# An attention layer with a feed-forward tail on one core: four heads at a time in the weighing, rounds of three score pairs and two units of fp32 work

## The reference

```python
h = layernorm(x) * (1 + ca) + sa
q = einsum('bnhd,hed->bnhe', h.reshape(B, N, 16, 16), Wq)
scores = einsum('bnhe,bmhe->bhnm', q, q) * 4      # / 16 ** -0.5
res = einsum('bhnm,bmhe->bnhe', softmax(scores), q)
x = x + ga * (res.reshape(B, N, 256) @ Wp.T + bp)
h = layernorm(x) * (1 + cb) + sb
# FFN: a second layernorm, w1 (256x1024, dequantised), silu, w2 (1024x256), residual
x = x + gb * (h + 0.5 * (silu((layernorm(h) * gamma + beta) @ w1 + b1) @ w2 + b2))
```

## Time and profile before

| | us |
|---|---|
| median of three runs | 2234.79 |
| profiled execution | 2229.72 |
| its span | 2227.4 |
| PE busy | 2010.8 (90%) |
| ACT busy | 1990.1 (89%) |
| DVE busy | 541.6 (24%) |
| mean granted clock of TensorE, share of full speed | 0.979 |

### The profile page before, as it was taken

The page is one execution under the profiler, slowest core; times in us unless marked ns, Lnnn a source line. Parts: engine busy times, 40 slices in busy tenths (PEclk is TensorE's granted clock), DMA queues, the critical chain, the costliest instruction groups (busy, mean ns, idle before and its releaser), DMA issues.

```text
span 2227.4 us, 34350 instructions
## 1 busy us (share of the span) xinstructions
PE 2010.8 (90%) x14087; PEld 598.4 (27%) x14087; DVE 541.6 (24%) x1289; ACT 1990.1 (89%) x2161; POOL 91.6 (4%) x42
## 2 busy tenths in 40 slices
PE   5578889899999999899998999999998999989995
PEld 3312222222322223222322223222332223222233
DVE  7513101421124211421014211322014211232113
ACT  2489999999998999999998999989998999989980
POOL 2000000100001000100001000000001000010001
PEclk9889999999999999999999999999999999999997
DMA  3251111111111111112111111111111111111000
GB/s 124 80 169 47 47 44 41 45 40 43 46 50 40 47 47 45 49 28 56 43 52 38 45 50 39 46 40 54 39 55 38 40 44 51 44 33 42 28 10 10
DMA packets 66572, 107.45 MB, mean 48 GB/s; under 512 B 15344, under 2 KB 49776, under 8 KB 66160
## 3 DMA queue, kind: packets, MB, share of 16 engines
q1 hardware_dynamic: 66416, 105.26, 16.2%
HBM read 96.56 MB, written 8.65 MB: 47 GB/s over the span
## 4 chain that ended last, share of the span: by engine, by line
PE 66%; ACT 15%; DVE 8%; issue 5%; DMA 0%; ACTq 0%; SPq 0%; DVEq 0%
PE attend_sums L700 34%; PE attend_scores L688 16%; ACT attend_probs L664 14%; PE attend_out L733 5%; PE attend_out L728 5%; DVE attend_sums_sb L818 3%; PE attend_sums L709 3%; PE attend_out L719 1%; ACT attend_half_tanh L653 1%; DVE attend_rsqrt_work L73 1%; DVE attend_rs L68 1%; PE attend_scores L728 1%; PE attend_scores L733 1%; DVE attend_st L847 1%; DVE z L873 0%
## 5 line engine op out<-in xcount | busy, mean ns | idle before, releaser
L664 ACT ACTIVATE attend_probs<-attend_scores 128x1024 f32<-128x1024 f32 x2048 | 1918.6, 1033 | 101.5 <-PE attend_scores L688 90.5
L700 PE MATMUL attend_sums<-attend_probs,values 128*17 128x512 f32 x8192 | 988.3, 600 | 0.2 <-ACT attend_probs L664 0.2
L688 PE MATMUL attend_scores<-asks,keys 64*128 64x512 f16 x4096 | 648.8, 384 | 85.3 <-ACT attend_probs L664 71.0
L688 PEld LDWEIGHTS attend_scores<-asks,keys 64*128 64x128 f16 x4096 | 151.6, 93 | 838.0 <-ACT attend_probs L664 681.8
L700 PEld LDWEIGHTS attend_sums<-attend_probs,values 128*17 128x17 f32 x8192 | 189.5, 97 | 467.2 <-issue 413.5
L818 DVE COPY attend_sums_sb<-attend_sums 128x512 f32<-128x512 f32 x128 | 88.5, 691 | 869.1 <-PE attend_sums L700 869.1
L733 PE MATMUL attend_out<-w,hidden 128*128 128x256 f32 x448 | 126.6, 405 | 0.0
L728 PE MATMUL attend_out<-attend_ffn_in,w 128*128 128x512 f32 x224 | 126.0, 645 | 0.0
L883 DVE TENSOR_SCALAR attend_half_in<-attend_out,b_col 128x512 f32<-128x512 f32 x56 | 42.0, 751 | 336.5 <-PE attend_out L728 336.5
L709 PE MATMUL attend_sums<-ident,attend_sums_sb 128*128 128x128 f32 x512 | 83.9, 286 | 35.3 <-DVE attend_sums_sb L818 35.3
L733 PEld LDWEIGHTS attend_out<-w,hidden 128*128 128x128 f32 x448 | 75.9, 189 | 45.1 <-issue 39.3
(11 more groups left out here) (130 smaller groups left out, 604.2 us busy)
## 6 DMA issues: line engine op xcount, KB each, us to landing
keys<-parts_dram SPq DMA_DIRECT2D x256, 128.0 KB
keys<-parts_dram SPq DMA_DIRECT2D x256, 64.0 KB
keys<-parts_dram SPq DMA_DIRECT2D x256, 56.0 KB
asks<-parts_dram SPq DMA_DIRECT2D x192, 64.0 KB
start_x_in<-L_attn_x SPq DMA_DIRECT2D x8, 512.0 KB, 6.3
parts_dram<-start_q_parts SPq DMA_DIRECT2D x16, 256.0 KB, 2.5
attend_x_now<-L_attn_x SPq DMA_DIRECT2D x8, 512.0 KB, 7.5
out<-attend_base SPq DMA_DIRECT2D x16, 256.0 KB, 5.8
```

Of the source, the lines that this page charges most:

```text
L664: act.activation(probs[n % P_RING], ps_scores[:, 2 * slot:2 * slot + 2, :], ACT.Exp, scale=scale)\
L688: last = pe.matmul(ps_scores[:, 2 * (n % S_RING) + b, :], keys[rows, hh % K_RING, j * P:(j + 1) * P], asks[rows, h, :], start=True, stop=True)
L700: last = pe.matmul(ps_sums[32 * q:32 * q + E1, :], values[:, tile, hh % H, :], probs[(4 * m + i) % P_RING][:, b, :], start=(d == 0 and i < ...
```

## The change

A *group* is now four heads, and the loop goes over 32 groups of 16 steps. A step is four pairs, one of each head, for the same two key tiles. The four column tiles of the weighing belong to the four heads. A *unit* is four matmuls, one for each head; two units make a step. Each tile then holds the complete sum of its head, so the addition of four quarters (L823) goes, and copy, transposes and division come once per group instead of once per head, with four heads in one division.

Keys come in parts: a part is a quarter of the keys of the four heads, and it takes eight DMAs where a head took six. `probs` has 12 slots.

TensorE's order is in rounds. A group of 64 pairs has 22 rounds, 20 of three pairs and two of two. Behind the pairs of a round stand two units of fp32 work: two units of the weighing in the even rounds, one unit and then one piece in the odd ones. Round 0 does the last two units of the group before, and round 1 has `turn_sums` and a piece. The pieces have 44 places per chunk instead of 48. Both norms are computed on VectorE directly after the last projection piece.

Below, `SIZES` are the pairs of each round, `UNITS` its units, `WEIGHED` their running sum.

```diff
+Q_HEADS = 4
+GROUPS = G * Q_GROUPS
+STEPS = TILES // 2
+PAIRS = STEPS * Q_HEADS
+S_RING, P_RING, K_RING = 3, 12, 4
+SIZES = [3] * 20 + [2] * 2
+UNITS = [0, 0] + [2 - r % 2 for r in range(2, len(SIZES))]
+PLACE_ROUND = range(1, len(SIZES), 2)
+TURN_ATT, PROJECT, TURN_Z2, UP, DOWN = 0, 2, 9, 11, 28
...
-                def weigh(m):
-                    hh, d = divmod(m, 4)
-                    if d == 0:
-                        pe.wait_ge(sums_cleared, 1) if hh == 0 else pe.wait_ge(quarters_added, hh)
-                    pe.wait_ge(exps_done, 4 * m + 4)
-                    for i in range(4):
-                        for b in range(2):
-                            q, tile = (2 * i + b) % 4, 4 * d + i + PAIRS * b
...
+                def weigh(gg, unit):
+                    j, b = divmod(unit, 2)
+                    if unit == 0:
+                        pe.wait_ge(sums_cleared, 1) if gg == 0 else pe.wait_ge(group_done, gg)
+                    if b == 0:
+                        pe.wait_ge(exps_done, gg * PAIRS + Q_HEADS * (j + 1))
+                    for hq in range(Q_HEADS):
+                        n = gg * PAIRS + Q_HEADS * j + hq
+                        last = pe.matmul(ps_sums[32 * hq:32 * hq + E1, :], values[:, j + STEPS * b, (gg % Q_GROUPS) * Q_HEADS + hq, :],
+                                         probs[n % P_RING][:, b, :], start=(unit == 0), stop=(unit == 2 * STEPS - 1))
+                    if b == 1:
+                        last.then_inc(steps_done, 1)
...
-                        if n % 2 == 0 and n >= P_RING:
-                            act.wait_ge(units_done, (n - P_RING) // 2 + 1)
+                        if n % Q_HEADS == 0 and n >= P_RING:
+                            act.wait_ge(steps_done, (n - P_RING) // Q_HEADS + 1)
...
-                for hh in range(HEADS):
-                    c, h = divmod(hh, H)
-                    for d in range(4):
-                        scores(hh, 4 * d)
-                        scores(hh, 4 * d + 1)
-                        if d == 1 and hh > 0:
-                            turn_sums(hh - 1)
-                        scores(hh, 4 * d + 2)
-                        if c > 0 and d != 1:
-                            out_piece(c - 1, slot_of(h, d))
-                        scores(hh, 4 * d + 3)
-                        if hh > 0 or d > 0:
-                            weigh(4 * hh + d - 1)
...
+                for gg in range(GROUPS):
+                    c, group = divmod(gg, Q_GROUPS)
+                    for r in range(len(SIZES)):
+                        for p in range(STARTS[r], ENDS[r]):
+                            scores(gg, p)
+                        if r == 0 and gg > 0:
+                            for unit in range(WEIGHED[-1], 2 * STEPS):
+                                weigh(gg - 1, unit)
+                        if r == 1 and gg > 0:
+                            turn_sums(gg - 1)
+                        for unit in range(WEIGHED[r] - UNITS[r], WEIGHED[r]):
+                            weigh(gg, unit)
+                        if r in PLACE_ROUND and c > 0:
+                            out_piece(c - 1, group * SLOTS + r // 2)
...
-                    dve.tensor_reduce(whole, ps_sums.rearrange("p (t q e) -> p t e q", t=GT, q=4)[:, :, 0:E1, :],
-                                      AX.X, ALU.add).then_inc(quarters_added, 1)
-                    dve.wait_ge(quarters_added, hh + 1)
-                    dve.reciprocal(inverse, whole[:, :, E]).then_inc(inverse_ready, 1)
...
+                    dve.reciprocal(inverse, turned[:, :, :, E]).then_inc(inverse_ready, 1)
```

More of the change, by code:

```diff
@@ L27 @@
 REACH = 120.0
[L29 to L33, removed]
-RSQRT_STEPS = 12
+Q_HEADS = 4
+Q_GROUPS = H // Q_HEADS
+GROUPS = G * Q_GROUPS
+STEPS = TILES // 2
+PAIRS = STEPS * Q_HEADS
+S_RING, P_RING, K_RING = 3, 12, 4
+K_STEPS = STEPS // 4
+K_PAIRS = K_STEPS * Q_HEADS
+FILL_K, FILL_Q = 16 * 8, 16 * 10
+RSQRT_STEPS = 12
+SIZES = [3] * 20 + [2] * 2
+ENDS = [sum(SIZES[:r + 1]) for r in range(len(SIZES))]
+STARTS = [0] + ENDS[:-1]
+UNITS = [0, 0] + [2 - r % 2 for r in range(2, len(SIZES))]
+WEIGHED = [sum(UNITS[:r + 1]) for r in range(len(SIZES))]
+PLACE_ROUND = range(1, len(SIZES), 2)
+SLOTS = len(PLACE_ROUND)
+TURN_ATT, PROJECT, TURN_Z2, UP, DOWN = 0, 2, 9, 11, 28
 class Scope:
@@ L385, in adaln_layer, with load_keys @@
             "shift_set", "shift_turned", "split_step", "shift_stored"))
-        def load_keys(eng, hh):
-            h, slot = hh % H, hh % K_RING
+        def load_keys(eng, part):
+            group, quarter = divmod(part, 4)
+            head, slot = (group % Q_GROUPS) * Q_HEADS, part % K_RING
             for b in range(2):
[L391 to L395, removed]
+                first = b * HALF + quarter * K_STEPS * P
+                by_head = parts_dram[:, head * E:(head + Q_HEADS) * E, first:first + K_STEPS * P].rearrange("s (h e) n -> s e h n", e=E)
+                rows = keys[64 * b:64 * b + 64, slot, :, :]
+                eng.dma_start(rows[0:E], by_head[0]).then_inc(k_in[slot], 16)
+                eng.dma_start(rows[E:2 * E], by_head[0]).then_inc(k_in[slot], 16)
+                eng.dma_start(rows[2 * E:3 * E], by_head[1]).then_inc(k_in[slot], 16)
+                eng.dma_start(rows[3 * E:3 * E + KEEP], by_head[1, 0:KEEP]).then_inc(k_in[slot], 16)
         def load_asks(eng, c, group):
@@ L550, in adaln_layer @@
         sums_sb = a.take("sums_sb", BANK)
-        inverse = a.take("inverse", GT)
-        whole = a.take("whole", GT * E1).rearrange("p (t e) -> p t e", t=GT)
+        inverse = a.take("inverse", GT * Q_HEADS).rearrange("p (t h) -> p t h", t=GT)
         st2 = a.take("st2", GT * 6).rearrange("p (t s) -> p t s", t=GT)
@@ L591, in _ @@
                 load_shifts(sp, 0, 0)
+                load_keys(sp, 2)
+                load_keys(sp, 3)
                 for group in range(1, Q_GROUPS):
-                    load_keys(sp, group + 1) if group + 1 < K_RING else None
                     load_asks(sp, 0, group)
@@ L606, in _ @@
                 load_x(sp, 0)
-                for hh in range(HEADS):
-                    c, h = divmod(hh, H)
[L609 to L615, removed]
+                for part in range(4 * GROUPS):
+                    sp.wait_ge(scores_ready, K_PAIRS * (part + 1))
+                    if part + K_RING < 4 * GROUPS:
+                        load_keys(sp, part + K_RING)
+                    c, within = divmod(part, 4 * Q_GROUPS)
+                    if within % 4 == 3 and c + 1 < G:
+                        load_asks(sp, c + 1, within // 4)
+                        load_shifts(sp, c + 1, within // 4)
+                    if within == 0 and c > 1:
                         sp.wait_ge(y_ready, 2 * (c - 2) + 2)
                         store_y(sp, c - 2, 1)
-                    if h == 8 and c > 0:
+                    if within == 8 and c > 0:
                         sp.wait_ge(x1_ready, 2 * c)
                         load_x(sp, c)
-                    if h == 13 and c > 0:
+                    if within == 14 and c > 0:
                         sp.wait_ge(y_ready, 2 * (c - 1) + 1)
@@ L665, in _ @@
                            .then_inc(exps_done, 1)
-                        if c > 0 and (h, j) in tanh_after:
-                            tanh(c - 1, tanh_after[h, j])
+                        if c > 0 and (group, p) in tanh_after:
+                            tanh(c - 1, tanh_after[group, p])
                 o = G - 1
@@ L676, in _, with scores @@
                 pe.wait_ge(kappa_set, 2)
[L678 to L684, removed]
+                def scores(gg, p):
+                    n = gg * PAIRS + p
+                    c, group = divmod(gg, Q_GROUPS)
+                    j, hq = divmod(p, Q_HEADS)
+                    part = n // K_PAIRS
+                    if n % K_PAIRS == 0:
+                        pe.wait_ge(k_in[part % K_RING], FILL_K * (part // K_RING + 1))
+                    if p == 0:
+                        pe.wait_ge(q_in[group], FILL_Q * (c + 1))
@@ L685, in scores @@
                     wait(pe, exps_done, n - S_RING + 1)
                     for b in range(2):
-                        rows = slice(64 * b, 64 * b + 64)
-                        last = pe.matmul(ps_scores[:, 2 * (n % S_RING) + b, :], keys[rows, hh % K_RING, j * P:(j + 1) * P],
-                                         asks[rows, h, :], start=True, stop=True)
+                        rows, col = slice(64 * b, 64 * b + 64), (j % K_STEPS) * P
+                        last = pe.matmul(ps_scores[:, 2 * (n % S_RING) + b, :], keys[rows, part % K_RING, hq, col:col + P],
+                                         asks[rows, group * Q_HEADS + hq, :], start=True, stop=True)
@@ L708, in turn_sums @@
+                def turn_sums(gg):
+                    pe.wait_ge(sums_copied, gg + 1)
                     for t in range(GT):
@@ L944, in _, with after_tanh @@
+                def after_tanh(o, s):
```

(2 more changed lines are left out.)

183 lines of the change are left out of this document (75 added, 108 removed).

## The result

| | before | after |
|---|---|---|
| median (4 runs each), us | 2233.44 | 2153.99 |
| range, us | 2229.79 to 2237.96 | 2153.62 to 2154.42 |
| span of the profiled execution, us | 2227.4 | 2151.0 |

The ratio is 0.9644, with a 95% interval of 0.9628 to 0.966: 79 us less, 3.6% faster. The forecast was 2140 (2105 to 2175).

The account below looks back on a forecast made before the run. By stage, PE bounded the chunks with pieces, an ACT-PE loop chunk 0. Seven chunks at 244.7 us plus 236.2 make 1949.1 against 2040.85, 91.7 less; 2229.7 - 91.7 = 2138, given as 2140, range 2105 to 2175.

Parts of the forecast that it names:

- Middle of a group: Double rounds of three pairs each, six exps: 5.70 us with a piece, 5.50 without; ACT idle about 0.2 us.
- step s: TensorE's step between unit and piece, shown by no row of before: taken as 0.11 us, between 0 and 0.30.
- free step: Step s at 0, its lower end; the sum would be some 18 us lower.
- dear one: Rival: step s at 0.30 us at some 31 places per chunk, 34 us more, 2174; chance 0.11.
- The seam: Rounds 20 and 21, two pairs each but full blocks: 4.25 us for the last four exps; 3.9 in a chunk's first group.
- From exp 58: Chain reckoned at the seam from this exp: 6.25 us for six exps, two (2.0) already counted, so 4.25 for four.
- The norm's wait: Once per chunk, the wait for the second norm (z2) and the low clock behind it, 4.8 us, would go.
- cover: From last projection piece to z2's first: 20.9 us, VectorE needing 19.1, so the norm is in time by 1.8 us.
- At nothing: DVE's copies, additions and divisions, 12 slots of `probs`, and two more DMAs per part were put at no cost.

Follow-up runs that it names:

- first experiment: Kernel before, with POOL's three additions for `base` started after the second norm instead of beside it: 2196.0 against 2232.9 us, ratio 0.9844.
- second against first: Second: kernel before, with copy, transposes and division of the sums only at every fourth head, 2191.5 us, ratio 0.9817; set against the first experiment.

## Why the prediction was right, and where it was off

The direction, the mechanism and the range were right; the gain was 79 us where 94 was forecast.

*Middle of a group: right.* 5.70 forecast and 5.71 measured with a piece, 5.50 and 5.51 without. The step s = 0.11 was measured as 0.11, so neither the free step nor the dear one came true. ACT's idle time in these double rounds is 0.10 us, at the first exp of a round, where about 0.2 was expected.

*The seam: the term that was mis-sized.* The prediction counted "From exp 58", that is, it let the second pair of round 20 wait for exp 58, as third pairs do. But a round of two pairs comes to this wait when exp 58 is over: in the group shown exp 58 ends at 594.70, the first pair starts at 595.29 and the second at 595.52. PE arrives late and not ACT. The right sum is PE's work alone, from figures that the prediction had: 0.54 + 1.84 + 0.54 + 2.04 = 4.96 for four exps instead of 4.25. The 0.71 in three groups and 0.34 in the first (4.24 for 3.9) make 2.5 of the 2.95 us by which a chunk missed, some 17 us in all. The rest is spread over the double rounds, such as the 5.77 behind each seam and, in the third group, rounds with a tanh. That PE has no pause in the timeline, and that one unit less takes its whole 0.86 from the seam, shows that this work is what counts there.

*The norm's wait: right*, in cause and nearly in size (4.5 for 4.8 per chunk). The cover of 2.0 us held. The weighing behind the wait is 1.76 times as long as usual (3.36 against 1.91), not quite doubled; the granted clock over it is 0.55 on average, so nearly all of it ran at the lower level.

*At nothing: right for what was said, but one thing was missed.* PE never waits for keys in the chunks; that the form of the old DMAs held up the store of the bounds, and that 3.5 us would be won before the first exp, I had not seen. By luck it made up for a part of the seam.

Taken apart by the runs, the 76.4 us of the two spans are: 31.5 for the norm's wait (first experiment), 9 for the turns (second against first: 6.4 and 2.6), 31 for rounds in threes in place of blocks of four (1761.9 to 1731.9 in chunks 1 to 7, 238.1 to 236.8 in chunk 0), 4 before the first exp, and under 1 in the tail. The order of the first two parts matters: rarer turns alone take away the norm's wait too, 41 us together, so in the changed kernel that wait may be gone by the grouping, by the moved norms, or by either. The third part is a difference of two kernels and holds the four-head order too; an order of rounds without the grouping was not tried. What the grouping brings by itself is therefore not shown.

Still open is why the changed kernel ran at 2154.0 in one set of runs and at 2158.0 in another, while the profiled executions of both (2153.6 and 2154.7) are nearly alike. In the second set two of the five are at 2154.6 and 2154.7 and three at 2158 to 2160.

## What to carry to other kernels

Where two engines feed each other through a short ring, write down the loop from a release over the block behind it to the next supply, and beside it the plain sum of the work; the larger one counted here at both places, and in the short rounds it changed from the loop (5.70 against a sum of 5.40) to the sum (4.96 against a loop of 4.25). A cost in a chain can be hidden by its neighbour's catching up, so take it out alone before crediting it. And look for the one wait with a low clock behind it first: here one moved semaphore in the kernel before brought 37 us, where the whole change brought 79.

## What the hardware showed that I had not expected

- Some small instructions on VectorE (128x4 elements) that take 0.17 us took up to 2.2 us while POOL ran an addition of 128x1024 elements (2.37 us each), and 0.17 again when POOL's work was moved. They are not slowed but held to the end: beside each of the 24 additions in the trace of either kernel, one such instruction ends 0.02 or 0.03 us after the addition does. The norm's statistics (L847, L851) run beside the first addition in their usual time.

```profile
418.06 2.38 POOL L641 TENSOR_TENSOR attend_base<-attend_base,b_gb 128x1024 f32<-128x1024 f32 x1
418.24 2.21 DVE L68 TENSOR_SCALAR attend_rs<-attend_rsqrt_work 128x4 int32<-128x4 int32 x1
```

- A full-array piece directly behind the transposes of the sums starts 542.57 - 542.08 = 0.49 us after them, where the way back to the scores takes 0.59. So the step of 0.10 is missing between two runs of fp32 matmuls on the whole array, while the changes of tiling in these traces cost 0.10 to 0.11 each. A unit takes 0.98 to the scores and 0.98 to a piece alike. The rule weighed in the prediction says that a change of tiling mode, and not a mere change of tile, drains TensorE (the Trainium skill, TensorEngine Tiling (Array Packing), Tiling Modes). The trace agrees as far as a cost goes: unit to piece has it though both are fp32, transposes to piece has not. The piece behind the transposes then takes 0.96 to the next scores (542.57 to 543.53) instead of 1.06, another 0.10, for which no run shows the reason; turn and piece together cost 1.45 us, and the prediction had 1.65.

```profile
542.08 0.66 PE L732 MATMUL attend_sums<-ident,attend_sums_sb 128*128 128x128 f32 x4
542.57 1.03 PE L756 MATMUL attend_out<-w,hidden 128*128 128x256 f32 x4
543.53 0.61 PE L712 MATMUL attend_scores<-asks,keys 64*128 64x512 f16 x4
```

- Two DMAs of 64 KB in place of one that writes its rows twice (128 KB) shortened the wait of a store queued behind them: 1.5 or 1.6 us in nine traces instead of 5.0 to 6.3 in four.
